# Routed attention with the sums two groups late, the maxima between the halves of a group's scores, and the values after them

## What is computed

```python
op = jnp.argmax(h[0, 0, :NOPS])
q, k, v = h @ wq[op], h @ wk[op], h @ wv[op]
attn = softmax(einsum('bqd,bkd->bqk', q, k) * scale)
y = einsum('bqk,bkd->bqd', attn, v) @ wo[op]
h = where(attn_mask[op], y, h)
z = relu(h @ w1[op] + b1[op]) @ w2[op] + b2[op]
h = where(ffn_mask[op], z, h)
```

## Time and profile before

| | us |
|---|---|
| median of three runs | 605.42 (604.44 to 605.49) |
| span of the profiled execution, first to last instruction | 599.8 |
| TensorE's granted clock, mean over the span | 0.948 of full speed |
| PE busy | 514.0 |
| the three attentions | within 410 to 568 of the span |

### The profile page before, as it was taken

The page is one execution under the profiler, slowest core; times in us unless marked ns, Lnnn a source line. Parts: engine busy times, 40 slices in busy tenths (PEclk is TensorE's granted clock), DMA queues, the critical chain, the costliest instruction groups (busy, mean ns, idle before and its releaser), DMA issues. The chain is left out here.

```text
span 599.8 us, 15533 instructions
## 1 busy us (share of the span) xinstructions
PE 514.0 (86%) x6332; PEld 297.7 (50%) x6332; DVE 409.6 (68%) x766; ACT 304.1 (51%) x526; POOL 159.1 (27%) x210
## 2 busy tenths in 40 slices
PE   7877678999897899798888789868999999999983
PEld 3556554466665642365555444415553655365420
DVE  5658978675444699787888758753665685658463
ACT  4136535233443300359888854353666555656473
POOL 1105423000000000405666500000780277038500
PEclk8556999999999979999999999998999999999998
DMA  7400006000000181000000000000000000000002
GB/s 251 46 1 3 3 3 230 1 2 1 2 1 2 37 202 45 2 1 1 3 1 2 3 20 0 7 14 1 2 3 10 2 2 2 11 2 1 2 6 75
DMA packets 22564, 15.09 MB, mean 25 GB/s; under 512 B 17465, under 2 KB 20569, under 8 KB 22362
## 3 DMA queue, kind: packets, MB, share of 16 engines
q1 hardware_dynamic: 22490, 14.00, 9.2%
HBM read 8.71 MB, written 1.08 MB: 16 GB/s over the span
## 5 line engine op out<-in xcount | busy, mean ns | idle before, releaser
L1978 ACT ACTIVATE R<-ps 128x512 f32<-128x512 f32 x96 | 52.1, 594 | 41.3 <-PE ps L1720 41.3
L2154 DVE TENSOR_REDUCE R<-ps 128x4 f32<-128x1024 f32 x48 | 56.5, 1209 | 18.4 <-PE ps L1706 18.1
L2062 POOL TENSOR_TENSOR R<-R 128x512 f32<-128x512 f32 x42 | 53.4, 1270 | 15.5 <-ACT R L1978 15.4
L1499 POOL TENSOR_TENSOR R<-R 128x512 f32<-128x512 f32 x32 | 45.4, 1418 | 43.2 <-DVE R L1433 43.2
L1720 PE MATMUL ps<-tmpA,R 32*128 32x256 f32 x384 | 49.2, 374 | 0.0
L1433 DVE TENSOR_TENSOR R<-ps,lasting 128x512 f32<-128x512 f32 x64 | 41.2, 685 | 11.7 <-PE ps L1359 11.7
L1706 PE MATMUL ps<-R,tmpA 32*128 32x256 f32 x384 | 48.0, 404 | 0.0
L1466 ACT ACTIVATE R<-R 128x1536 f32<-128x1536 f32 x32 | 47.3, 1479 | 0.1
L1359 PE MATMUL ps<-R,Q 32*128 32x128 f32 (+1 forms) x512 | 29.9, 346 | 10.0 <-ACT R L1482 10.0
L1720 PEld LDWEIGHTS ps<-tmpA,R 32*128 32x128 f32 x384 | 36.3, 185 | 1.0
L2046 POOL TENSOR_TENSOR R<-R 128x8 f32<-128x8 f32 x24 | 5.0, 208 | 116.5 <-DVE R L2154 116.5
(11 more groups left out here) (322 smaller groups left out, 1100.5 us busy)
## 6 DMA issues: line engine op xcount, KB each, us to landing
R<-z SPq DMA_DIRECT2D x32, 128.0 KB, 2.3
R<-in_qv SPq DMA_DIRECT2D x1, 2560.0 KB
x<-in_x SPq DMA_DIRECT2D x4, 256.0 KB, 3.5
out<-x SPq DMA_DIRECT2D x4, 256.0 KB, 3.7
lasting<-in_lasting SPq DMA_DIRECT2D x1, 811.0 KB, 7.8
early<-in_early SPq DMA_DIRECT2D x1, 793.5 KB, 7.1
scatter<-in_scatter SPq DMA_DIRECT2D x1, 512.0 KB, 5.5
P<-scratch_w SPq DMA_DIRECT2D x16, 32.0 KB, 2.4
```

The lines of the kernel that those rows point to most:

```text
L1499: pool.tensor_tensor(diagonal(u), diagonal(u), diagonal(u), ALU.mult).then_inc(diag_squared[1], 1)
L1978: act.activation(m.et[:, g % 2, j, :], ps[:, turned_bank(g, j), :], ACT.Exp)\
L2062: pool.tensor_tensor(m.esum[:, g % 2, two, :], m.et[:, g % 2, two, 0:N], m.et[:, g % 2, two, N:2 * N], ALU.add).then_inc(sg["halves_added" ...
L2154: dve.tensor_reduce(m.parts[:, g % 2, :, a:a + 2, 3 * g].rearrange("p s i -> p i s"), ps[:, a:a + 2, :].rearrange("p i (s m) -> p i s m", ...
```

## The change

On PE the order within a group becomes: first half, sums of g-2, maxima of g+1, second half, values of g-1. The sums of the groups 6 and 7 are both made from the exponentials, at the end, ahead of the last values. The banks move with it: the turned maxima lie in bank 6 from group 2 on, the last two groups' sums in the banks 7 and 4, the last values in bank 5, and the second quarter of the token values in bank 6. New waits go with the banks: values(g) waits until the maxima of g+2 are copied out (`m_copied`), invert(g) until the maxima of g+3 are turned, the feed-forward for the last sums and for the last product at its second chunk. On DVE invert(g-2) now stands ahead of copy_maxima(g+1) and spread_inverses(g-2) behind maximum(g+2, 1). ACT's `keep` moves behind all four exponentials of a group; the last group needs none, since DVE multiplies straight from PSUM. POOL splits g+2 between its two additions of group g.

```diff
     def m_ps(g):
-        return ps[:, 7 if g == 0 else 2, 0:N // 2].bitcast(BF16)
+        return ps[:, (7, 2)[g] if g < 2 else 6, 0:N // 2].bitcast(BF16)
+    SUMMED = G - 2
+    def sums_at(g):
+        if g < SUMMED:
+            return ps[:, 6, N:2 * N]
+        return ps[:, 7, N:2 * N] if g == SUMMED else ps[:, 4, 0:N]
+    def values_at(g):
+        return ps[:, 6 if g < G - 1 else 5, 0:N]
...
                 def maxima(g):
                     pe.wait_ge(sg["parts"], 2 * (g + 1))
-                    if 1 <= g < G - 1:
+                    if g == 1:
                         pe.wait_ge(sg["max_done"], scored(g + 1, 0))
+                    if g == 2:
+                        pe.wait_ge(sg["vt_copied"], NCH)
...
                 def values(g):
                     pe.wait_ge(sg["exp_done"], J * (g + 1))
-                    if g >= 1:
+                    if 1 <= g < G - 1:
                         pe.wait_ge(sg["sums_turned"], g)
+                    if g + 2 < G:
+                        pe.wait_ge(sg["m_copied"], g + 3)
...
                 def sums(g):
-                    pe.wait_ge(sg["y_kept"], g + 1)
-                    if g < G - 1:
+                    if g < SUMMED:
+                        pe.wait_ge(sg["y_kept"], g + 1)
                         pe.wait_ge(sg["halves_added"], 2 * (g + 1))
...
                     else:
+                        pe.wait_ge(sg["exp_done"], J * G - 2 if g == SUMMED else J * G)
...
-                    token_values(1, 5)
-                    pe.wait_ge(sg["vt_copied"], 2)
+                    token_values(1, 6)
+                    pe.wait_ge(sg["vt_copied"], 1)
                     for g in range(G):
                         pair_turned(g, 0)
                         if g == 0:
+                            pe.wait_ge(sg["vt_copied"], 2)
                             token_values(2, 6)
-                        elif g == 1:
-                            pe.wait_ge(sg["vt_copied"], NCH)
-                        if g >= 1:
-                            values(g - 1)
+                        else:
+                            if g >= 2:
+                                sums(g - 2)
+                            if g + 1 < G:
+                                maxima(g + 1)
                         pair_turned(g, 1)
                         if g == 0:
+                            maxima(1)
                             pe.wait_ge(sg["vt_copied"], 3)
                             token_values(3, 6)
-                        if g + 1 < G:
-                            maxima(g + 1)
-                        if g >= 1:
-                            sums(g - 1)
+                        else:
+                            values(g - 1)
+                    sums(G - 2)
+                    sums(G - 1)
                     values(G - 1)
-                    sums(G - 1)
...
                         pe.wait_ge(sg["y_made"], min(2 * k + 2, G - 1))
-                        if k == NCH - 1:
+                        if k == 1:
+                            pe.wait_ge(sg["sums_turned"], G)
                             pe.wait_ge(sg["y_last"], 1)
...
                     pe.wait_ge(sg["y_made"], 1)
+                    pe.wait_ge(sg["sums_turned"], G - 1)
...
                         if k == 1:
-                            pe.wait_ge(sg["y_kept"], G)
-                            pe.wait_ge(sg["sums_turned"], G)
+                            pe.wait_ge(sg["y_kept"], G - 1)
...
# ACT
-                            if g >= 1 and j == 1:
-                                keep(g - 1)
-                    keep(G - 1)
+                        if g >= 1:
+                            keep(g - 1)
# POOL
-                    add_halves(0, 0)
-                    for g in range(1, G):
-                        add_halves(g - 1, 1)
-                        if g + 1 < G:
-                            split(g + 1)
+                    for g in range(G):
+                        if g < SUMMED:
                             add_halves(g, 0)
-                        if g >= 2:
-                            normalise(g - 2)
+                        if g >= 3:
+                            normalise(g - 3)
+                        if g + 2 < G:
+                            split(g + 2)
+                        if g < SUMMED:
+                            add_halves(g, 1)
+                    normalise(G - 3)
                     normalise(G - 2)
# DVE
                     def invert(g):
                         dve.wait_ge(sg["sums_ready"], g + 1)
-                        dve.transpose(m.sumt[:, :], ps[:, 6, N:2 * N]).then_inc(sg["sums_turned"], 1)
+                        if g + 3 < G:
+                            dve.wait_ge(sg["m_ready"], g + 4)
+                        dve.transpose(m.sumt[:, :], sums_at(g)).then_inc(sg["sums_turned"], 1)
...
-                            dve.wait_ge(sg["y_kept"], g + 1)
-                            dve.tensor_tensor(h[:, g * N:(g + 1) * N], m.yz[:, g, 0:N], m.yz[:, g, N:2 * N],
+                            dve.wait_ge(sg["pv_ready"], g + 1)
+                            dve.tensor_tensor(h[:, g * N:(g + 1) * N], values_at(g), m.yz[:, g, N:2 * N],
                                               ALU.mult).then_inc(sg["y_last"], 1)
...
                         if g + 2 < G:
                             maximum(g + 2, 0)
                         if g >= 2:
-                            spread_inverses(g - 2)
+                            invert(g - 2)
                         if g + 1 < G:
                             copy_maxima(g + 1)
-                        if g >= 1:
-                            invert(g - 1)
                         if g + 2 < G:
                             maximum(g + 2, 1)
+                        if g >= 2:
+                            spread_inverses(g - 2)
+                    invert(G - 2)
                     spread_inverses(G - 2)
                     invert(G - 1)
                     spread_inverses(G - 1)
```

More of the change, by code:

```diff
@@ L1765, in values @@
                             at = (2 * g + t) * 128 + 32 * j
-                            mm = pe.matmul(ps[rows_of(j), 6, 0:N], vtok[:, at:at + 32],
+                            mm = pe.matmul(values_at(g)[rows_of(j), :], vtok[:, at:at + 32],
                                            m.et[:, g % 2, j, t * N:(t + 1) * N], start=(t == 0), stop=(t == S - 1))
@@ L1770, in sums @@
                 def sums(g):
-                    pe.wait_ge(sg["y_kept"], g + 1)
-                    if g < G - 1:
+                    if g < SUMMED:
+                        pe.wait_ge(sg["y_kept"], g + 1)
                         pe.wait_ge(sg["halves_added"], 2 * (g + 1))
                         for j in range(J):
-                            mm = pe.matmul(ps[rows_of(j), 6, N:2 * N], m.ones32[:, :], m.esum[:, g % 2, j, :],
+                            mm = pe.matmul(sums_at(g)[rows_of(j), :], m.ones32[:, :], m.esum[:, g % 2, j, :],
                                            start=True, stop=True)
                     else:
+                        pe.wait_ge(sg["exp_done"], J * G - 2 if g == SUMMED else J * G)
                         for t in range(S):
                             for j in range(J):
-                                mm = pe.matmul(ps[rows_of(j), 6, N:2 * N], m.ones32[:, :],
+                                mm = pe.matmul(sums_at(g)[rows_of(j), :], m.ones32[:, :],
                                                m.et[:, g % 2, j, t * N:(t + 1) * N], start=(t == 0), stop=(t == S - 1))
@@ L1965, in attention @@
                     act.activation(m.mrow[:, 0, :], m_ps(0), ACT.Copy).then_inc(sg["m_copied"], 1)
-                    copy_values(1, 5)
+                    copy_values(1, 6)
                     def keep(g):
@@ L1976, in attention @@
                                 act.wait_ge(sg["pv_ready"], g - 1)
-                                act.wait_ge(sg["halves_added"], 2 * (g - 1))
+                                act.wait_ge(sg["halves_added"], 2 * min(g - 1, SUMMED))
                             act.activation(m.et[:, g % 2, j, :], ps[:, turned_bank(g, j), :], ACT.Exp)\
@@ L2052, in normalise @@
                     pool.wait_ge(sg["inv_done"], g + 1)
+                    if g == SUMMED:
+                        pool.wait_ge(sg["y_kept"], g + 1)
                     pool.tensor_tensor(h[:, g * N:(g + 1) * N], m.yz[:, g, 0:N], m.yz[:, g, N:2 * N],
```

## The result

Timed side by side, the changed kernel runs at 0.9918 of the kernel before, 95% interval 0.9889 to 0.9948. On the 605.42 us of before that is 600.5 us, 5.0 us less (3.1 to 6.7); the forecast was 602.9, and the range ended at 601.0. The direction was right and the gain larger than forecast.

A forecast was written before the change was run, and what follows sets the result against it. PE was taken to bound inner groups (4.15 of 4.15 us), leaving only 2.24 us of waits an attention, at its ends, to win. 3 x 0.95 - 0.3 = 2.55 us turned 605.42 into 602.9, range 601.0 to 605.0.

The forecast's parts named there:

- Head: From an attention's start to group 1: waits for token values and copied maxima go, group 1 starts 1.16 us earlier.
- Group 1: Second half's second shift waits 0.42 us for the group's first exponential; the group lasts 4.00 us.
- some 0.1: In group 1, the us allowed for the second shift beyond 1.18 + 0.22, putting it at 1.5 after the group's start.
- the stall of group 7: Ahead of group 7's second half, a wait of 0.07 us for its exponential (1.93 against 1.86).
- Groups 2 to 5: Values wait 0.15 us a group for DVE's copy of the maxima, bounds 0.05 and 0.29; 0.60 us given back.
- End: From group 7 to the feed-forward: 7.00 us against 7.23, with sums of 6 and 7 at 1.00 each.
- the rival on the seams: PE drains at new tile-shape changes around the maxima: 4.1 us slower, 609.8 with the waits; chance 0.10.
- The cover of the second chunk: In the feed-forward after an attention, the second chunk's wait for DVE's last product is covered by some 0.7 us.
- Feed-forwards: All five get one more wait ahead of their first matmul, at most one release of 0.06; 0.3 us in all.
- DVE end to end: No overlap on DVE: values wait 0.29 us in twelve groups, 1.7 us more, 604.6; chance 0.14.
- nothing won: Idle time at the attention's ends moves behind another wait (last product, exponentials): 605.4; chance 0.08.
- The rival of no wait on DVE's copy: Groups 2 to 5 lose 0.05 us or nothing: 601.1 to 601.7; chance 0.13.

The follow-up runs named there:

- r5: Kernel before with only the second quarter of token values in bank 6 and maxima of group 1 earlier; attention 38.06 us against 39.20, no ratio.
- r7: Changed kernel plus four needless matmuls between the halves of group 1; group 1 took 4.16 us against 4.12, no ratio.
- r2: Changed kernel with DVE's copy of the maxima ahead of its inversion; ratio 0.9878 to the kernel before, groups 2 to 5 4.16 us each against 4.31.
- three comparisons: Changed kernel against the kernel before, timed three times without further edit: ratios 0.9918, 0.9958 and 0.9923.
- r4: Kernel before timed against itself, no edit; ratio 1.0004 (0.9967 to 1.0041).
- r9: Kernel before with the change's head and end but not its new order in the groups; ratio 0.9882, attention 37.29 us.
- r10: Changed kernel with DVE's copy ahead of the inversion and group 6 summed from POOL's halves; ratio 0.9868 to the kernel before, attention 37.06 us.

## Why the prediction was right and wrong

Every wait that was forecast is there, and the gain comes from the ends; of the sizes the end was furthest off, and the sum was 0.7 us short of the 3.3 in the attentions.

*Head.* Forecast 1.16 won, 1.15 measured; alone (r5) 1.14.

*Group 1.* A new stall of 0.42 for its own exponential was forecast, a group of 4.00; the stall is 0.50 and the group took 4.12. r7 and the trace show the cause. The exponential and its release were right, 1.94 after the group's start where I had 1.93; wrong was the "some 0.1" by which I let the second shift stand behind the first. Where nothing waits, the two start within 0.01 of each other (533.54 both). The same 0.1 makes the stall of group 7 0.18 in place of 0.07.

*Groups 2 to 5.* Forecast 4.30, measured 4.31. The term that had no row before, 0.15 us between 0.05 and 0.29, was right in its cause, which r2 shows by removing it. That its size came out is in part luck: the copy took 0.24 where I had 0.29, and its release 0.15 where I had 0.06, and with 0.01 less in each of three other terms these errors cancel. That the transpose would start ahead of the maximum's recorded end was right: it starts at 539.99, 0.08 ahead of 540.07. The section of the Trainium skill that I cited against the change ("VectorE: DVE Perf Modes", "The DRAIN you can't avoid") would, by the sentence I took from it, have made the wait 0.29; it adds that a next instruction that is not held starts earlier, which I left out; the trace agrees with that, by these 0.08. Group 6: 4.15 forecast, 4.16 measured.

*End: the step that failed.* I gave the feed-forward's start 7.00 us from group 7; it took 6.70. "Then sums of 6 and of 7, from the exponentials: 1.00 each" took that price from a row in which the sums follow a wait and precede another tile shape. Behind the values they cost (564.79 - 563.07) / 2 = 0.86 each, and the values of 6 ahead of them 0.89. Four steps of one shape in a row pay the change of shape once: 0.28 us less for the sums and 0.13 for the values, of which the longer stall of group 7 takes 0.11 back. The rule I cited for the rival on the seams, that changing the tiling mode drains TensorE ("TensorEngine Tiling (Array Packing)", "Tiling Modes"), agrees with this trace, in which a step ahead of another shape takes 0.11 us more (1.00 against 0.89), and I used it only where it spoke against the change, not where it spoke for it. 0.3 x 3 = 0.9 us. The cover of the second chunk is thinner than the 0.7 us forecast: the last product ends at 566.85, 0.49 ahead of that chunk at 567.34.

*Feed-forwards.* 0.3 us for one more wait in each was the upper bound; it costs nothing that the trace shows. From the first matmul of the third feed-forward to that of the next, which has no attention, it is 12.31 us in both kernels (568.09 to 580.40 before, 565.77 to 578.08 after).

Together: 2.55 + 0.9 + 0.3 - 3 x 0.12 gives 3.4, measured 3.3. What the first comparison showed beyond that, up to 5.0, is within what three comparisons leave open; a range set by the terms alone, ending at 601.0, had no room for the measurement's own spread, which I put at 0.2% and which is 0.3% either way in the first comparison and 0.37% in r4.

*Rivals.* DVE end to end is out by the 4.31 us of the groups 2 to 5, the seams are out by r2; nothing won is out by every stretch. The rival of no wait on DVE's copy didn't occur, but r2 shows what it would have been worth.

And one thing the forecast did not ask: whether the parts belong together. The new order inside the groups, which names the change, costs 0.62 - 0.04 us an attention there and 0.23 at the end, and the gain is all at the ends (r9). What the order adds is that the sums of 6 can stand at the end and hide the wait for the last exponentials; with DVE's copy put first and POOL's halves used, the attention is 0.23 us shorter than with both ends alone (r10 against r9; 0.20 of it lie from group 7 on).

## What to carry to other kernels

When an engine is busy for the whole of a steady stage, a new order of the same work has little to win inside it (here 0.11 us for a change of tile shape that it saves) and new waits to lose by; price these waits by following the late engine's queue instruction by instruction, and look for the gain at the stage's two ends. An edit that reorders several queues should be taken apart and each part run alone: here the part that gave it its name was the one that cost. And where the span spreads more than the change is worth, find a stretch inside it that repeats to two hundredths and measure there.

## What was not expected of the hardware

A step takes about 0.11 us more where a group of another tile shape follows: values to sums stand 0.89 apart, values to a half 1.00. The weights and what is multiplied change with the shape, and no run takes these apart.

A release reaches PE at different prices: 0.06 us after DVE's copy in the kernel before (535.86 to 535.92) and after an exponential in the changed one (535.42 to 535.48), but 0.15 after DVE's copy in the groups 2 to 5 of the changed one (540.82 to 540.97). The trace shows what lies in between: a semaphore instruction of its own on PE's queue, for the last of the waits that stand ahead of the values (L1778), from 540.86 to 540.91, then the first weights at 540.94. The profile's line for it (its length in ns, its start rounded):

```profile
L1778 PEldq EVENT_SEMAPHORE  x1: 51/51/51, 540.9 to 540.9; - x1
```

Ahead of the two shifts at 0.06 there is none. The last values of the kernel before have one too (L1762, 565.42 to 565.47) and start 0.12 after the exponential's end at 565.41. No run moves such a wait, so that it is the price of the instruction is read from these places and not tested.

And the same program can run the same last stretch in 31.71 or in 35.15 us, with the mean granted clock at 0.92 or 0.79; in the changed kernel's profile it was down to half, 1.2 GHz, from 580 to 585 us, after PE had been idle for 1.64 us ahead of the first matmul at 578.08. The profile before has the same idle time there and kept its clock; what decides it is open.
